# Adjacency-masked attention plus a graph attention layer on one core: five probs slots, probs slots freed by context and sums apart, one shared parts buffer for key and query, and a new order of work

## The reference

```python
h = relu(layernorm(x))
q, k, v = (h @ W.T + b for Wq, Wk, Wv)          # 4 heads of 32, keys in 8 chunks of 128
scores = clip(q @ k.T / sqrt(32), -10, 10)
scores = where(adj == 0, -10, scores)
attn = softmax(scores, axis=-1)                  # over the 128 keys of one chunk, each chunk alone
ctx = sum over chunks of attn @ v                # divided by each chunk's own sum
x = x + layernorm(ctx @ Wo.T + bo + h) * gamma + beta
h = relu(layernorm(x))
Wh = h @ W ; e = leaky_relu(Wh@a1 [i] + Wh@a2 [j], 0.2); e = -inf where no edge
x = x + elu(softmax(e) @ Wh)
```

## Time and profile before

| | |
|---|---|
| median of 3 runs | 799.07 us (797.36 to 800.09) |
| profiled execution | 797.73 us, span 796.0 us |
| PE busy | 730.7 us, 92% |
| DVE busy | 689.5 us, 87% |
| ACT busy | 616.9 us, 77% |
| POOL busy | 547.1 us, 69% |
| mean granted clock | 0.97 of 2.4 GHz |

### The profile page before, as it was taken

How to read it: one execution, slowest core, us unless ns; L and a number is a source line. 1 busy time by engine, 2 the same in 40 slices (tenths; PEclk the granted TensorE clock), 3 DMA queues, 4 the chain that set the end, 5 groups by cost and what they waited for, 6 DMA issues and landing times. The chain is left out here.

```text
span 796.0 us, 14906 instructions
## 1 busy us (share of the span) xinstructions
PE 730.7 (92%) x5075; PEld 432.8 (54%) x5075; DVE 689.5 (87%) x1172; ACT 616.9 (77%) x1060; POOL 547.1 (69%) x634
## 2 busy tenths in 40 slices
PE   5799999999999999999999999999999999767666
PEld 3434454454556646475557546554557445556656
DVE  3889899899999999999999999999989998766562
ACT  5798887978898898889888898689886888336434
POOL 2007363657886888788796988677875899677273
PEclk9799999999999999999999999999999999977969
DMA  8443221413212152213412322302320201120111
GB/s 276 148 173 114 85 91 31 159 67 123 78 62 97 61 161 74 87 54 113 147 32 70 107 97 102 100 27 93 133 78 31 88 26 47 41 62 5 41 27 40
DMA packets 58650, 68.60 MB, mean 86 GB/s; under 512 B 5328, under 2 KB 35024, under 8 KB 58576
## 3 DMA queue, kind: packets, MB, share of 16 engines
q1 hardware_dynamic: 57568, 67.39, 25.1%
q10 hardware_dynamic: 1008, 0.26, 0.1%
HBM read 21.50 MB, written 12.58 MB: 43 GB/s over the span
## 5 line engine op out<-in xcount | busy, mean ns | idle before, releaser
L1455 DVE SCALAR_TENSOR_TENSOR probs<-score,cap 128x1024 f32<-128x1024 f32 x256 | 308.1, 1212 | 24.8 <-ACT score L1291 22.3
L1291 ACT ACTIVATE score<-score 128x1024 f32<-128x1024 f32 x256 | 257.0, 1014 | 47.4 <-PE score L1628 45.9
L1219 POOL TENSOR_TENSOR gathered<-gathered,scaled 128x512 f32<-128x512 f32 x112 | 159.6, 1425 | 79.4 <-DVE scaled L1480 78.7
L1628 PE MATMUL score<-query_stack,key_stack 128*128 128x512 f32 x512 | 187.7, 453 | 5.4 <-DVE probs L1455 4.7
L1244 POOL TENSOR_TENSOR ring<-ring,see_t 128x512 f32<-128x512 f32 x112 | 146.4, 1320 | 25.7 <-DVE ring L1543 25.7
L1640 PE MATMUL ctx_ps<-probs,value 128*32 128x512 f32 x1024 | 136.1, 603 | 0.4 <-ACT context L1300 0.4
L1649 PE MATMUL sum_ps<-probs,one_of 128*32 128x512 f32 x1024 | 134.2, 596 | 0.0
L1720 PE MATMUL work<-wh,ring 128*128 128x130 f32 x1024 | 128.3, 282 | 4.8 <-ACT ring L1370 4.1
L1720 PEld LDWEIGHTS work<-wh,ring 128*128 128x128 f32 x1024 | 125.7, 197 | 10.1 <-issue 4.5
L1628 PEld LDWEIGHTS score<-query_stack,key_stack 128*128 128x128 f32 x512 | 80.0, 190 | 67.0 <-DVE probs L1455 40.7
L1370 ACT ACTIVATE ring<-ring,wh 128x512 f32<-128x512 f32 x128 | 88.5, 723 | 7.5 <-POOL ring L1244 4.0
(11 more groups left out here) (115 smaller groups left out, 952.1 us busy)
## 6 DMA issues: line engine op xcount, KB each, us to landing
key_stack<-key_parts SPq DMA_DIRECT2D x64, 256.0 KB, 2.5
query_stack<-query_parts SPq DMA_DIRECT2D x64, 256.0 KB, 2.6
x_in<-in_x SPq DMA_DIRECT2D x16, 256.0 KB, 3.4
h_kept<-x_in SPq DMA_DIRECT2D x16, 256.0 KB, 2.8
res<-h_kept SPq DMA_DIRECT2D x16, 256.0 KB, 2.8
h<-in_x SPq DMA_DIRECT2D x16, 256.0 KB, 3.2
x_kept<-res SPq DMA_DIRECT2D x16, 256.0 KB, 2.0
gat_x<-x_kept SPq DMA_DIRECT2D x32, 128.0 KB, 2.4
```

Of the source, the lines that this page charges most:

```text
L1219: nc.gpsimd.tensor_tensor(gathered[:, :, :], gathered[:, :, :], scaled[:, k % SCALED], ALU.add).then_inc(gathered_step, 1)
L1291: nc.scalar.activation(some, some, ACT.Exp, scale=DH ** -0.5).then_inc(exp_done, 1)
L1455: nc.vector.scalar_tensor_tensor(out=probs[:, step % 2, h:h + GROUP, :], in0=score[:, h:h + GROUP, :], scalar=LOW, in1=caps.broadcast_to([ ...
L1628: last = nc.tensor.matmul(score[:, head, :], key_stack[:, head, chunk * P:(chunk + 1) * P], query_stack[:, head, half * HALF:(half + 1) * ...
```

## The change

It has four parts: `probs` becomes five slots of one group each; a group's write waits for both context and sums of the step that last read its slot (five groups back); key and query share one `parts` buffer, except the key of batch 0, which uses two blocks of `ring`, and the ACT copies wait in a chain query 0, key 0, key 1, query 1; and all tables of places are new. The engines' instructions and their number stay the same.

```diff
+KEPT = 5
-        key_parts = sb("key_parts", [P, 2, HALF], F32R)
-        query_parts = sb("query_parts", [P, 2, HALF], F32R)
+        parts = sb("parts", [P, 2, HALF], F32R)
-        probs = sb("probs", [P, 2, HEADS, HALF])
+        probs = sb("probs", [P, KEPT, GROUP, HALF])
+        def of_head(b, k, h):
+            return probs[:, group_of(b, k * STEP_GROUPS + h // GROUP) % KEPT, h % GROUP, :]
+        def parts_of(is_key, b):
+            return ring[:, CHUNKS:CHUNKS + 2, :].bitcast(F32R) if is_key and b == 0 else parts[:, :, :]
+        def parts_before(is_key, k, b):
+            if b == 0:
+                return (is_key, 0, 0) if k else None
+            if is_key:
+                return (k == 1, 0, b)
+            return (True, 1, b) if k else (False, 1, b - 1)
...
                 elif name == "query" or name == "key":          # ACT
-                    before = (keys_stacked if is_key else queries_stacked)[1 - k]
-                    wait(act, before, (b + k) * 64)
+                    before = parts_before(is_key, k, b)
+                    if before:
+                        act.wait_ge((keys_stacked if before[0] else queries_stacked)[before[1]], (before[2] + 1) * 64)
...
                 if name == "probs":                             # DVE
+                    used = (group_of(b, k) - KEPT) // STEP_GROUPS
+                    if h == 0 or KEPT % STEP_GROUPS:
+                        wait(dve, sums_done, used + 1)
+                        wait(dve, context_done, used + 1)
                     if h == 0:
-                        wait(dve, sums_done, step_of(b, step) - 1)
...
-                        out=probs[:, step % 2, h:h + GROUP, :], in0=score[:, h:h + GROUP, :], scalar=LOW,
+                        out=probs[:, group_of(b, k) % KEPT], in0=score[:, h:h + GROUP, :], scalar=LOW,
```

More of the change, by code:

```diff
@@ L43 @@
     0: {
[L44 to L64, removed]
-    },
-    1: {
[L67 to L85, removed]
-    },
@@ new lines @@
+        "key": [-23518, -836],
+        "value": [-11130, -3074],
+        "turn_sums": [7103, 11897],
+        "gather": [7536, 7691, 8116, 8431, 9103, 9126, 9885, 9933, 12582, 12738, 13213, 13693, 13806, 14563, 14590,
+            14929],
+        "turn_context": [10991, 15689],
+        "project": [13005, 17399],
+        "turn_hidden": [15279, 19929],
+        "to_row": [17767, 20218],
+        "wh": [22093, 22524, 23237],
+        "near_row": [24614, 25707],
+        "base_row": [24621, 24730],
@@ new lines @@
+    4: {
+        "scores": [1215, 1654, 1866, 1868, 2494, 2551, 2828, 2959, 3567, 3569, 4590, 4762, 5519, 5718, 5789, 5903,
+            6205, 6238, 7017, 7667, 7842, 8033, 8161, 8375, 8767, 8824, 8993, 9120, 9500, 9919, 10572, 10576],
+        "context": [2072, 2632, 2878, 4104, 4930, 5846, 6075, 6248, 7555, 8065, 8325, 8967, 9137, 10287, 10733,
+            11120],
+        "sums": [2241, 2758, 2841, 4055, 5622, 5880, 6533, 6825, 7853, 8162, 8231, 8929, 9144, 10454, 10740, 11082],
+        "turn_x": [-3888, -939],
+        "query": [-1906, 5105],
+        "key": [-664, 1088],
+        "value": [255, 3303],
+        "turn_sums": [7833, 11528],
+        "gather": [7902, 8084, 8596, 8978, 9468, 9920, 10470, 10847, 12176, 12565, 12990, 13064, 14220, 15046, 15396,
+            15794],
+        "turn_context": [12096, 16648],
+        "project": [12231, 17956],
+        "turn_hidden": [16052, 21885],
+        "to_row": [21926, 22011],
+        "wh": [24442, 24920, 25153],
+        "near_row": [25459, 26448],
+        "base_row": [25513, 27000],
+        "share": [29300, 29358, 30202, 30478, 34956, 34983, 35043, 35072],
+    },
@@ new lines @@
+        "query": [-55939, -611],
+        "key": [-52955, -1500],
+        "turn_sums": [5258, 9739],
+        "gather": [6567, 7222, 7605, 7694, 8326, 8703, 9175, 9550, 9816, 9924, 10528, 11209, 12215, 13830, 14394,
+            14746],
+        "project": [10337, 16663],
+        "stats_y": [10672, 16761],
+        "moments_y": [10838, 17112],
+        "invert": [28377, 30081, 32639, 33396],
+        "stats_x": [-210812, -40439],
+        "moments_x": [-203522, -22478],
+        "stats_z": [13317, 17701],
@@ L803 @@
[L803 to L821 removed]
+        "load_x": [13716, 13488],
```

1329 lines of the change are left out of this document (665 added, 664 removed).

## The result

The changed kernel takes 776.40 us (median of 4, 775.67 to 777.40), the kernel before 798.26 us (4, 797.36 to 800.09): ratio 0.9717, 95% interval 0.9702 to 0.9732. The profiled execution took 776.54 us with a span of 774.8 us, 21.2 us less than the 796.0 of before. A gain was forecast, of 8.5 us; it is about 22.

A forecast was written before the change was run, and what follows sets the result against it. PE was taken as the limit from 40 to 660 us, a dependent chain at the end. Middle 0, start 0, end -2.0 - 2.0 - 1.6 - 2.9 = -8.5 us gave 791 us, range 781 to 801.

The forecast's parts named there:

- The order within the middle: PE from 40 to 660 us: the new lists leave its work and holes alike; 0, bounds -10.5 and +10.5 us.
- Five probs slots: DVE's old wait for sums was 0.8 us in all, so the slot by itself is worth 0 to 0.8; taken as 0.
- the first rival: The fifth slot also empties PE's holes in the middle: 6 to 10 us below 791, 781 to 785 us; chance 0.12.
- Pairs on PE: Untying sums from context in PE's middle leaves changes of matmul form nearly equal (302 and 300): 0.2 us less, taken as 0.
- One parts buffer: ACT's key copy waits for the query's stack, but it fits: cost 0, at most 1 us in each of 7 batches.
- the slower rival: The key copy stands on ACT for the query's stack, near 2 us a batch: 805 us; chance 0.15, including new middle holes.
- The end of attention: Only sums[15] and one to_row stand between the last probs and turn_sums: -2.0 us, bounds 0 and -3.
- gather and rows: Batches 7 and 6: gather13 and 14 ahead of the rows, near_row6[0] right behind base_row6[0]; -2.0 us, bounds 0 and -5.3.
- apply_y7[1]: On ACT in GAT 6, it goes ahead of below6[0] instead of waiting behind it: -1.6 us, bounds 0 and -5.9.
- The last GAT: Batch 7's end: base_row ahead of near_row, hide7[1] earlier, only leaky7[15] and its hide behind invert; -2.9 us, bounds 0 and -4.
- The prediction's own signs: Checks: PE busy within 3 us in the middle, 5 in total; to_row6[0] within 3 of 675.26; named waits gone or absent.

The follow-up runs named there:

- e3: Changed kernel with four probs slots in place of five and sums[12] of batch 3 moved ahead of gather[4]: 788.87 us, ratio 0.9870 to the kernel before.
- e13: Changed kernel, five slots kept, with only sums[12] of batch 3 moved ahead of gather[4] on PE: 777.35 us, ratio 0.9710 to the kernel before.
- e4: Changed kernel with each context that stood behind its sums moved right ahead of them on PE: 793.09 us, ratio 0.9917 to the kernel before.
- e7: Kernel before, old lists adapted, with both waits, one shared parts buffer and five slots: 811.02 us, ratio 1.0146 to the kernel before.
- e6: Kernel before, old lists adapted, with both waits and one shared parts buffer, four slots: 806.01 us, ratio 1.0087 to the kernel before.
- e9: Kernel before with the new lists only from the last scores to the row transposes of GAT 6: 792.95 us, ratio 0.9914.
- e12: Kernel before with one ACT item moved, apply_y7[1] ahead of below6[0]: 801.47 us, ratio 1.0006.
- e10: Kernel before with the new lists only from the start of GAT 6's leaky to the first peaks7: 796.74 us, ratio 0.9960.
- e11: Kernel before with the new lists only from the first peaks7 to the end: 796.24 us, ratio 0.9956.
- e5: Kernel before with DVE also waiting for context_done beside sums_done: 802.59 us, ratio 1.0035.
- e8: Changed kernel with only the one wait that can be unmet kept, on every other group: 776.14 us, ratio 0.9706 to the kernel before.
- e1: Kernel before's four slots and buffers with both waits, old lists to the last scores, new lists behind: 787.03 us, ratio 0.9842 to the kernel before.
- e15: Changed kernel with hide6[13] and hide6[15] ahead of invert6[1] on DVE and only the wait that can be unmet: 775.47 us, ratio 0.9693 to the kernel before.
- e14: Changed kernel with hide6[13] and hide6[15] moved ahead of invert6[1] on DVE: 775.74 us, ratio 0.9699 to the kernel before.
- e2: Kernel before's four slots and buffers with both waits, new lists to the last scores (sums[12] of batch 3 moved), old behind: 803.44 us, ratio 1.0052.

## Why the prediction missed

**The order within the middle, taken as 0 (bounds -10.5 and +10.5): the step that failed.** The argument that "the same kind of list with the same items" would leave the same holes didn't hold, and neither did the one that PE's work stays the same to within a microsecond. The last scores come 10.5 us earlier as a mean over five traces each, at the edge of the bound: 6.1 us less idle time and 4.4 us less busy time of PE. Between 40 and 660 us the changed kernel's holes are 5.64 us where 10.55 stood. Of the busy time 0.6 us is turn_hidden6[1], four transposes that now stand behind the last scores. Most of the rest hangs on the slot and not on the neighbours in the list: with the same list PE is busy 646.57 us with four slots (e3) and 643.10 with five (e13), while one matmul lasts the same in both (scores 448 ns, context 599, sums 600), so that the 3.5 us are in how far consecutive matmuls overlap. What in the list makes it use the slot was not separated, but for the place of context (e4).

**Five probs slots, taken as 0 (bounds 0 to 0.8): not contradicted for the slot by itself, and misread for the change.** Under the old list the slot gives nothing (e7 against e6, with the reserve about e7's waits). But the small wait was also held against the first rival, and there the reading failed. That list was one that four slots can serve; its small wait says that the list fits the buffer, not that the buffer is no limit to another list. Under the new list taking the slot away costs 12 us (e3 against e13). The step said that what the slot allows is another order, and then costed that order without the slot. The first rival had this mechanism and a fair price (6 to 10 us), at a chance of 0.12.

**Pairs on PE: right as to the pairs.** Context to sums costs 0.88 us again (318.05 to 318.93), and the untied sums broke no pairs that count. What untying brings wasn't in the prediction: context waits for ACT's copy of the one before, and a list that can put sums first gets round it. Tied again in this list, the kernel loses 16 us, of which that wait is 8 (e4). The rule of the Trainium skill (TensorEngine Tiling (Array Packing), Key Properties) that a change of tiling mode drains TensorE was thus no argument against this change. The trace agrees with it as far as going on to an item of another form takes 0.97 to 1.00 us from start to start, where one of the same form takes 0.88.

**One parts buffer: right as to the changed kernel,** where ACT has no wait for a stack of the query. Under the old list the waits come, 5.3 us in e7, so the slower rival's mechanism exists and the changed kernel, with its new places of key and query, doesn't have it. That rival's price was worked out too high: 7 + 4 + 3 us against 8 + 4.7 leaves 1.3 us a batch, not 2, and so 9 us in seven batches and 800 us, not 805. What the prediction didn't see is what the buffer is for. A slot is 4 KB per partition, as much as one of the two parts buffers held, and both kernels allocate the same 226520 bytes per partition: the parts buffer that goes pays for the slot. Whether five slots fit beside two parts buffers was not tried. Of the parts of the change that were each costed at nothing, list and slot gain only together (10.5 us).

**The end of attention, -2.0; measured -3.1.** The step named 2 to 3 us. The 1.45 us wait before to_row6[0] is gone too. It stood right behind scores7[31] and context7[14]; now sums7[14] and sums7[15] stand between as well, and PE starts them at 667.57 without a wait.

**gather and rows, -2.0; measured -4.8,** within its bound of -5.3, the whole wait of DVE. With e9 the two together are -7.0 us of time. The bound was the better guess: nothing else came in its place. Which of the moved items gives it was not separated.

**apply_y7[1], -1.6; measured -3.9 for the stretch, and 0 for the step (e12).** The size was too small and the reason was wrong: the item isn't on the chain to turn_hidden7[1]. What gives the 3.2 us of e10 is the new order of the items between the rows and peaks7 taken together; which of them was not separated.

**The last GAT, -2.9; measured -2.4** in the profile and -3.7 (-2.0 to -5.0) in e11. The swapped rows give what they were to give (0.7): from the end of POOL's last row_shift to the first leaky7 it is 2.12 us in the changed kernel and in e11, and 2.74 in the kernel before and in e12. The wait of 1.54 us before the last matmuls is gone, as forecast.

**The prediction's own signs.** PE busy from 40 to 660 us came out 4.9 us off where 3 were allowed, PE's total busy time 7.6 us lower (723.1 against 730.7) where 5 were, and to_row6[0] 5.9 us early (669.40) where 3 were. These three point at the middle, where 4.4 us of the busy time went. turn_sums7[1] 2.1 us behind the last probs, apply_y7[1] ahead of below6, the last share without a wait and ACT without a wait for the query's stack came as forecast.

The middle's mean of -10.5 and the end's -14.2 make 24.7 us, where the medians differ by 21.9 (798.26 to 776.40); the difference is of the size of the scatter of one profile. Of the miss of 14.6 us (791 to 776.4), about 10 are then the middle and 5 the end, each to within some 3 us. Among the terms of the end the nearest was the last GAT; apply_y7[1] was right in sign only.

## What to carry to other kernels

- A wait row prices a buffer only for the order that it was measured under. If the order changes with the buffer, size the buffer's worth by the holes of the engine that limits (here 10.5 us), not by its waits (0.8 us), and give that case a real chance. Even this isn't a strict bound: the gain of 10.5 us was 6.1 us of idle time and 4.4 us of busy time, and that it equals the holes of before is chance.
- Parts of a change that each look like nothing may be conditions of one another: here one more slot, and an order that uses it. Measure them in a table of two by two (list by slots), not one after the other.
- A wait ahead of an item says little on what moving it will bring. Follow the chain back from the next fixed point (here turn_hidden7[1]) and see whether the item is in it at all.

## What the runs showed of the hardware

- Waits on DVE that are met already went with a loss of 2.8 us (0.35%, 0.16 to 0.55%) in one order of work (e5: 126 waits more, one instruction more by the profile's count), and with none in another (e8: 376 waits and 125 instructions fewer, 776.14 against 776.40 us). What the trace of the first shows is PE waiting 8.0 us for probs where it was 4.7 us; why was not settled.
- The same 32 matmuls of 128x130 (share6[4,5]) took 3.81 us at a granted clock of 1.00, and 5.46 or 5.47 us where it was 0.69 as a mean over them (5.18 us at 0.73 in the changed kernel). With the new order there they were slow after 2.99, 2.37, 2.32, 2.27, 2.27 and 2.10 us of idle (changed kernel, e13, e1, e3, e8, e10), and at the full clock after 2.10, 2.03 and 1.94 us (e4, e15, e14). With the old order the last gap is 0.3 us in all, and they were slow in one (before) and at the full clock in six (e2, e5, e6, e7, e9, e11); e12, whose gap is 3.17 us, was slow. So a longer gap mostly went with the lower clock, and the gap alone doesn't decide it: 2.10 and 0.32 us are on both sides.
- Executions of the same old middle reach the last scores between 672.1 and 675.2 us, of the same new middle between 662.5 and 665.2. A single pair of profiles can be off by 3 us in 670, more than many of the steps costed here.
